# A transformer layer on one core: the rotated queries go through the DMA transpose without their duplicate, and VectorE duplicates them on the transposed side

## What is computed

```python
xn = layernorm(h)
q, k, v = xn @ Wq, xn @ Wk, xn @ Wv          # 32 heads of 32 for q, 8 groups for k and v
q, k = rope(q), rope(k)
scores = q @ k.T / sqrt(32), causal          # each k group serves 4 heads
h = h + softmax(scores) @ v @ Wo
z = layernorm(h)
h = h + 2 * sum_e(8 * softmax(z @ Wr + br)_e * (z @ A_e @ B_e))
```

## Time and profile before

| | us |
|---|---|
| median of three runs | 2368.4 (2367.73 to 2368.97) |
| profiled execution, its own time | 2369.94 |
| its span, first to last instruction | 2368.1 |
| mean granted clock of TensorE | 0.985 of full speed |
| layer stage, one pass in the steady part | 32.07 |

### The profile page before, as it was taken

The page is one execution under the profiler, slowest core; times in us unless marked ns, Lnnn a source line. Parts: engine busy times, 40 slices in busy tenths (PEclk is TensorE's granted clock), DMA queues, the critical chain, the costliest instruction groups (busy, mean ns, idle before and its releaser), DMA issues.

```text
span 2368.1 us, 58968 instructions
## 1 busy us (share of the span) xinstructions
PE 2259.8 (95%) x18704; PEld 1250.6 (53%) x18704; DVE 1889.4 (80%) x7794; ACT 1840.5 (78%) x6301; POOL 1710.4 (72%) x1529
## 2 busy tenths in 40 slices
PE   3998689999999999999999999999999999999986
PEld 2787245555555555555555555555555555555543
DVE  8999568788788887878878878888787887887864
ACT  7998478777887777787777788777778777778872
POOL 2544288787787777777778778777777777877871
PEclk9999899999999999999999999999999999999987
DMA  3888488899899999998999999998999998998983
GB/s 99 265 242 267 125 146 171 177 175 173 173 176 167 176 175 172 176 175 169 173 174 175 173 174 177 166 176 173 174 176 175 172 167 176 175 173 174 169 151 83
DMA packets 1192387, 410.10 MB, mean 173 GB/s; under 512 B 1150598, under 2 KB 1152902, under 8 KB 1192076
## 3 DMA queue, kind: packets, MB, share of 16 engines
q1 hardware_dynamic: 1192072, 406.33, 86.8%
q10 hardware_dynamic: 4, 0.00, 0.0%
HBM read 53.84 MB, written 67.11 MB: 51 GB/s over the span
## 4 chain that ended last, share of the span: by engine, by line
PE 85%; DVE 1%; ACT 1%; DMA 1%; POOL 1%; issue 0%; SPq 0%; POOLq 0%; DVEq 0%; ACTq 0%
PE pb L956 14%; PE pa L956 14%; PE pc L956 14%; PE s_ps L969 5%; PE pa L943 5%; PE pa L942 5%; PE pa L944 5%; PE pb L942 5%; PE pb L944 5%; PE pb L943 5%; PE pv_ps L987 2%; PE pd L987 2%; PE pd L942 1%; PE pd L944 1%; PE pd L943 1%; ACT pr L1110 1%
## 5 line engine op out<-in xcount | busy, mean ns | idle before, releaser
L1110 ACT ACTIVATE pr<-pr,smin 128x128 f32<-128x128 f32 x2048 | 793.1, 389 | 182.9 <-DVE smin L1256 182.7
L1475 POOL TENSOR_TENSOR pr<-pr,rinv 128x512 f32<-128x512 f32 x512 | 577.0, 1137 | 422.8 <-DVE rinv L1264 412.4
L1483 POOL TENSOR_TENSOR p<-pr,p 128x512 f16<-128x512 f32 x512 | 590.9, 1158 | 13.0 <-ACT p L1120 5.4
L1256 DVE CUSTOM_DVE_ANT_0 pr<-s_ps,cst 128x128 f32<-128x128 f32 x2048 | 468.8, 286 | 97.4 <-PE s_ps L969 59.3
L1120 ACT ACTIVATE p<-pr 128x512 f16<-128x512 f32 x512 | 318.8, 623 | 160.7 <-POOL pr L1475 137.3
L1110 ACT ACTIVATION_READ_ACCUMULATOR pr<-pr,smin 128x1 f32 x2048 | 384.3, 188 | 0.0
L956 PE MATMUL pa<-wkv_hi,xt 128*128 128x512 f16 x1024 | 326.5, 380 | 23.7 <-DMA xt<-xs 23.7
L956 PE MATMUL pb<-wq_hi,xt 128*128 128x512 f16 x1024 | 326.8, 380 | 1.2 <-DVE rows L1374 1.2
L956 PE MATMUL pc<-wq_hi,xt 128*128 128x512 f16 x1024 | 324.8, 379 | 0.0
L694 PE MATMUL hps<-z,xw 128*128 128x256 f32 x848 | 188.8, 383 | 50.0 <-POOL xw L381 36.2
L969 PE MATMUL s_ps<-kt,qt 128*128 128x128 f16 x2048 | 199.0, 220 | 9.4 <-DVE smin L1256 5.1
(11 more groups left out here) (203 smaller groups left out, 4897.3 us busy)
## 6 DMA issues: line engine op xcount, KB each, us to landing
h<-rows SPq DMA_DIRECT2D x128, 256.0 KB, 3.6
out<-rows SPq DMA_DIRECT2D x64, 512.0 KB, 2.9
rows_in<-h SPq DMA_DIRECT2D x38, 512.0 KB, 4.5
h_ln<-h SPq DMA_DIRECT2D x25, 512.0 KB, 4.4
pt<-p SPq DMA_TRANSPOSE x512, 3.6
xa<-x SPq DMA_DIRECT2D x16, 256.0 KB, 3.9
xb<-x SPq DMA_DIRECT2D x32, 128.0 KB, 3.6
wst<-wq SPq DMA_DIRECT2D x8, 512.0 KB, 5.5
```

Source lines behind the costliest of these rows:

```text
L1110: last = A.activation(p, p, ACT.Exp, bias=smin[g % 2][:, j:j + 1], scale=-1.0, accum_out=rsum[g % 2][:, j:j + 1])
L1256: V.tensor_tensor_reduce(pr[g % 2][:, cols], s_ps[g % 2][:, cols], mask, 1.0, 3e38, ALU.add, ALU.min, smin[g % 2][:, j:j + 1]).then_inc(ma ...
L1475: nc.gpsimd.tensor_tensor(p3, p3, rinv[g % 2][:, :].unsqueeze(2).broadcast_to([P, HG, P]), ALU.mult).then_inc(p_norm, 1)
L1483: nc.gpsimd.tensor_tensor(p[:, HG * P:], pr[g % 2][:, :], p[:, 0:HG * P], ALU.subtract).then_inc(pl_done, 1)
```

## The change

The high and low part of each head stay side by side in `qs` (64 columns a head, 1024 a half), and the DMA transpose of a half has 1024 columns. Two heads then land in one 128 by 128 square: an even head on partitions 0 to 63, the odd one behind it on partitions 64 to 127, in the even head's place in `qt`. Behind the landing VectorE makes three copies, each of 64 partitions by 8 heads by 128 columns: the odd head to partitions 0 to 63 of its own place, the same to partitions 64 to 127 of its own place, and, after a wait for these two, the even head from partitions 0 to 63 to 64 to 127. TensorE waits for `qt_done` in place of the landing. The second half's transpose is issued one pass earlier, behind k_transpose(i+1, 0) and ahead of `store`; the first half's copies stand behind router_weights, the second half's behind reciprocals(i+1, 0).

```diff
-        qs = sb("qs", [P, H, 2, 2, HD], f16)
+        qs = sb("qs", [P, H, 2, HD], f16)
...
                 def q_transpose(b, half):
                     if not has(b):
                         return
-                    reached(sp, qd_done, 2, b, half + 1)
+                    reached(sp, qh_done, 2, b, half + 1)
+                    reached(sp, ql_done, 2, b, half + 1)
                     reached(sp, s_done, G, b - 1, G // 2 * (half + 1))
-                    heads = slice(H // 2 * half, H // 2 * (half + 1))
-                    sp.dma_start_transpose(qt[:, heads, :],
-                                           qs[:, heads, :, :, :].rearrange("p h a b d -> p (h a b d)")
+                    h0_, h1_ = H // 2 * half, H // 2 * (half + 1)
+                    sp.dma_start_transpose(qt[:, h0_:h1_:2, :],
+                                           qs[:, h0_:h1_, :, :].rearrange("p h b d -> p (h b d)")
                                            ).then_inc(qt_in[half], 16)
...
                     k_transpose(i, 1)
-                    q_transpose(i, 1)
                     p_transpose(i, 0)
...
                     k_transpose(i + 1, 0)
+                    q_transpose(i + 1, 1)
                     store(i - 3)
...
                     if g % (G // 2) == 0:
-                        reached(pe, qt_in[g // (G // 2)], 16, b, 16)
+                        reached(pe, qt_done, 2, b, g // (G // 2) + 1)
                         reached(pe, kt_in[g // (G // 2)], 16, b, 16)
...
-                    reached(dve, qh_done, 2, b, half + 1)
-                    reached(dve, ql_done, 2, b, half + 1)
-                    part = qs[:, 16 * half:16 * half + 16, :, :, :].rearrange("p h a b d -> p h a (b d)")
-                    V.tensor_copy(part[:, :, 1, :], part[:, :, 0, :]).then_inc(qd_done, 1)
+                    reached(dve, qt_in[half], 16, b, 16)
+                    even, odd = (slice(16 * half + n, 16 * half + 16, 2) for n in range(2))
+                    V.tensor_copy(qt[0:2 * HD, odd, :], qt[2 * HD:4 * HD, even, :])
+                    V.tensor_copy(qt[2 * HD:4 * HD, odd, :], qt[2 * HD:4 * HD, even, :]).then_inc(qt_moved, 1)
+                    reached(dve, qt_moved, 2, b, half + 1)
+                    V.tensor_copy(qt[2 * HD:4 * HD, even, :], qt[0:2 * HD, even, :]).then_inc(qt_done, 1)
...
                     reciprocals(i, 5)
-                    q_double(i + 1, 0)
                     q_rotate(i + 1, 1)
...
                     router_weights(i - 2)
+                    q_double(i + 1, 0)
                     norm_refine(0, i + 3)
...
                     mask_min(i + 1, 0)
                     mask_min(i + 1, 1)
+                    reciprocals(i + 1, 0)
                     q_double(i + 1, 1)
-                    reciprocals(i + 1, 0)
```

More of the change, by code:

```diff
@@ L802, in layer_stage @@
         lsl_done = sem("lsl_done")
-        qd_done = sem("qd_done")
+        qt_moved = sem("qt_moved")
+        qt_done = sem("qt_done")
         kd_done = sem("kd_done")
@@ L1166, in q_high_a @@
                     reached(act, qt_in[0], 16, b)
-                    A.activation(qs[:, 0:16, 0, 0, :], qr[:, :].rearrange("p (h d) -> p h d", d=HD),
+                    A.activation(qs[:, 0:16, 0, :], qr[:, :].rearrange("p (h d) -> p h d", d=HD),
                                  ACT.Copy).then_inc(qh_done, 1)
@@ L1174, in q_high_b @@
                     reached(act, qt_in[1], 16, b)
-                    A.activation(qs[:, 16:32, 0, 0, :], qr[:, :].rearrange("p (h d) -> p h d", d=HD),
+                    A.activation(qs[:, 16:32, 0, :], qr[:, :].rearrange("p (h d) -> p h d", d=HD),
                                  ACT.Copy).then_inc(qh_done, 1)
@@ L1499, in q_low @@
                     reached(pool, qh_done, 2, b, half + 1)
-                    part = qs[:, 16 * half:16 * half + 16, 0, :, :]
+                    part = qs[:, 16 * half:16 * half + 16, :, :]
                     nc.gpsimd.tensor_tensor(part[:, :, 1, :], qr[:, :].rearrange("p (h d) -> p h d", d=HD),
```

## The result

The changed kernel takes 2512.5 us (median of four runs, 2511.3 to 2513.1) against 2368.7 for the kernel before (four runs, 2367.7 to 2370.0): 1.061 times as long, 95% interval 1.0597 to 1.0623.

A forecast was written before the change was run, and what follows sets the result against it. TensorE's gapless matmul stream was taken to bound the kernel. Stalls of 1.6 and about 1.0 us, 2.65 a pass over 61 passes, gave 160 us more: 2528 us, range 2400 to 2575, forecast's chance 0.50.

The forecast's parts named there:

- The bound and the due times: TensorE streams matmuls without a gap; scores(i+1, 0) stalls if `qt` is ready after about 1238.0; `ctx_t` has 0.63 us spare.
- GpSimd and VectorE taking turns: In the first half, copies into `qt` alternate with GpSimd's p_low and v_low, a waiting copy ending about 0.28 us behind.
- Rival 1: Two VectorE copies in a row keep GpSimd out: 1.6 us a pass in all, 2466 us; chance 0.17.
- Rivals 2 and 3: Copies do not wait for GpSimd: 2405 to 2441 us if the 8-column instruction still does (0.14), otherwise 2368 (0.10).
- Rival 4: A copy that moves between partitions takes 1.2 us: about 7.4 us a pass, 2820 us; chance 0.05.
- Rival 5: TensorE never waits for the copies, and lighter queues help ahead of 330 and behind 2280 us: 2363 us; chance 0.04.
- The 8-column instruction: On VectorE ahead of the first half's copies: starts about 0.31 us earlier and no longer waits for GpSimd's p_low.
- The first stall: At scores(i+1, 0), TensorE waits for the third copy into `qt`: matmul at 1239.75 instead of 1238.14, 1.6 us.
- The second stall: At the first output projection, VectorE's late ctx_low delays `ctx_t`: about 1.0 us added, 2.65 us late in all.
- the anchor: Point in VectorE's timeline, at 1224.17, where it idles 1.79 us for TensorE; its remaining lag dies there.
- The sum: 61 passes at 2.65 us make 162, taken as 160; added to the profiled 2369.9 gives 2530, as median 2528 us.
- SP and DMA: Half's transfer falls from 4.4 to 3.3 us and the second half's transpose moves ahead of store: no cost, no gain.

## Why the prediction was right

- **The bound and the due times** held. TensorE had no slack, both places where it was said to wait are the two and only places where it does, and the passes pay for them one by one.
- **GpSimd and VectorE taking turns** held in each pair of instructions. Rival 1 (two copies in a row keep GpSimd out) falls: v_low got its turn between the first and the second copy. Rivals 2 and 3 (copies of 64 partitions do not wait) fall by the lengths of 0.80 to 1.26 us, and by the run with GpSimd narrowed, where the same copies take 0.42. Rival 4 (slow between partitions) falls by the same 0.42. Rival 5 would have needed the lighter queues to help, and they are worth nothing.
- **The 8-column instruction** came free as worked out, 0.23 instead of 1.17; it saved VectorE 0.94 us a pass. It came free by 0.10 us, where the prediction had reckoned 0.15, and the three passes in which it did not have a first stall some 0.3 us longer, as the upper bound of the forecast had it. That it did so in nearly every pass rests on a small margin.
- **The first stall** was forecast at 1.6 and is 1.28. The term that was mis-sized is GpSimd's part of the turns: I let v_low end 0.62 behind the first copy and p_low 1.11 behind the second; they end 0.54 and 1.01 behind (1234.95 and 1236.24). TensorE's matmul starts 0.06 behind the third copy, not 0.14, and GpSimd had moved up by 0.21 where I took 0.16. That is 0.31 of the 0.32.
- **The second stall**, forecast near 1.0, is 0.90. The stretch from the masks' end to the second reciprocal, forecast at 3.2 us, is 3.23 (1239.12 to 1242.35). What is left of VectorE's lag dies at the anchor, as said: VectorE still idles 1.1 us there for TensorE, 1.8 before.
- **The sum**: 61 x 2.65 was taken. The 24 passes from 408.8 to 1232.9 us take 34.34 us on average, 2.27 more than before: 61 x 2.27 = 138, and some 5 us come from the stretches at the start and end, which I had put at nothing (near the end, where the chain of one block is not hidden behind others, TensorE waits 7.3 us for `qt` once, 4.3 in the kernel before at that point, and then 4.7 us for `ctx_t`, 1.1 before). 2528 forecast, 2512.5 measured. The pass alone was forecast 0.38 us too long, 23 us over the run; that the total is off by only 16 is in part luck, since the stretches left out go the other way.
- **SP and DMA** cost nothing and gave nothing. The run with the traffic put back shows it for the traffic. For the new order on SP the run with the second half alone in GpSimd's idle time shows it: its transpose is issued in the new place, and the time is 2371.0.

## What to carry to other kernels

An elementwise copy has no price of its own while another engine holds what it needs: the three copies here take 1.3 us where GpSimd idles and 3.0 where it does not, and for both halves the place decided between 0.8% and 6.1% of the kernel's time. Before work is moved onto VectorE, lay its timeline beside GpSimd's and look for instructions whose length swings between a short and a long value; those show the turns. And where one engine is busy without a gap, write down for each operand how long before its use it is ready. Here that margin was 0.63 us at `ctx_t`, and traffic saved on queues that nobody waits for could not pay for copies that used it up.

## What the runs showed of the hardware

A VectorE instruction whose partitions start elsewhere than those of the one ahead of it does not start before that one ends: the first copy starts at 1233.46 behind an end at 1233.43, the second at 1234.43 behind 1234.41, and norm_refine at 1236.56 behind 1236.53, whereas in the kernel before an instruction's record began 0.08 ahead of the end of the last (1237.45 against 1237.53). The rule that the prediction cites from the Trainium skill, *VectorE: DVE Perf Modes*, "Two Vector instructions with no wait between them", says this, and the trace agrees. The price here is about 0.1 us at each border.

Between VectorE and GpSimd the one that had been waiting went first in every case seen, also between two instructions queued back to back on the other side (v_low between the first and the second copy, the second copy between v_low and p_low). No copy into `qt` took over 1.42 us in any of these runs, less than its own 0.42 and one p_low of 1.16 together; none waited for two GpSimd instructions in a row.
